# Another order of the work between two token blocks in the expert stage of a gated cross-attention and mixture-of-experts kernel

## The chip, the core and the metric

The kernel runs on one core of one Trainium2 chip. Its engines work side by side, each through its own list of instructions, and meet only at semaphores: TensorE (PE) multiplies matrices, VectorE (DVE) and GpSimd (POOL) do element-wise work, ScalarE (ACT) evaluates activation functions, SyncE (SP) issues the transfers. The metric is device time in microseconds, the median of repeated executions. A separate execution was recorded by the hardware profiler, and all rows below come from it.

## The reference, cut to what matters

A first stage (attention) makes `x` of 4096 tokens by 128. The change is in the second stage, the expert layer:

```
w = gate weights per token and expert, thresholded and normalised
h = gelu(einsum('td,edf->etf', x, W1) + b1[:, None, :])     # 8 experts, 512 hidden
eo = einsum('etf,efd->etd', h, W2) + b2[:, None, :]
out = einsum('te,etd->td', w, eo)
x = x + tanh(g_ffn[0]) * out
```

## The kernel before, in words

The expert stage goes through the tokens in NB = 8 blocks of 512. A block has CH = 32 chunks: chunk `j` is expert `e = j // 4` and quarter `f = j % 4` of its 512 hidden features. Operands are kept as a rounded part and a remainder (`_high`, `_low`), so every product takes three matmuls of 512 columns.

For each chunk there is a **first group** on PE (L1060 to L1062, three matmuls into `ps_h`, one of four buffers `j % 4`), then ACT's gelu into `h_sb` (L627, counted by `h_done`) and, for even chunks, a second gelu that writes `h_high` (L632, counted by `high_even`). DVE makes `h_high` for odd chunks by a copy (L836, `high_odd`) and `h_low` for both chunks of a pair by a subtraction (L840, `low2_done`). Then comes the **second group** on PE, `second` (L1040 to L1042), which adds the chunk's three products into `ps_y`. LAG = 4: `second(g, j - 4)` stands right behind the first group of chunk `j`. I call a first group with the second group behind it a slot.

When the four second groups of an expert are done, DVE's `combine(g, e)` (L828) adds the bias and multiplies with the token weights from `w_row`: expert 0 goes straight into `yT`, the others into `weighted`, and for these POOL adds `weighted` to `yT` (L527, counted by `added`). After the last addition of a block PE turns `yT` by four transposes (`untranspose`, L1048, into `ps_t`) and DVE's `finish` (L815) adds the residual and makes `y_out`, which SP stores.

The order on each engine is the order in which the code is written. In the kernel before, a block ends with its last four second groups back to back (chunks 28 to 31, L1067) and, on DVE, with the last two combinations (L851). The next block begins with the first groups of its chunks 0 to 3 back to back; behind the first group of chunk 2 stand the transposes of the block before, and behind DVE's pair (2, 3) stands `finish`. Blocks 0 and 1 are written out, blocks 2 to 7 are one hardware loop (`loop_b`), in which the numbers that a wait compares with are computed in registers.

The first group of chunk `j` waits for `h_done` of chunk `j - 4` from chunk 4 on. For chunks 0 to 3 the line reads

```
wait_count(pe, h_done, g * CH + (j - 3) if j >= 4 else g * CH)
```

which for chunk 0 of a block means all 32 gelus of the block before.

Of the kernel before, what the change touches and what calls it, by code (L numbers as in the profile page):

```python
# [37 lines left out]
E, FF = 8, 512  # L38
# [6 lines left out]
FC = FF // P  # L45
CH = E * FC
BT = 512
NB = TOK // BT
TPB = BT // P
LAG = 4  # L50
# [43 lines left out]
def gated_block(nc, a):  # L94
# [3 lines left out]
    with ctx:  # L98
# [3 lines left out]
        def sem(name):  # L102
            return ctx.enter_context(nc.semaphore(name))
# [168 lines left out]
        weighted_done = sem("weighted_done")  # L272
# [29 lines left out]
        def wait_count(eng, s, n):  # L302
            if not (isinstance(n, int) and n <= 0):
                eng.wait_ge(s, n)
# [20 lines left out]
        def loop_b(eng, body):  # L325

            body(0)
            body(1)
            with eng.Fori(2, NB) as g:
                body(g)  # L330
# [307 lines left out]
        def _(dve):  # L638
# [172 lines left out]
            def finish(g):  # L811

                dve.wait_ge(t_full, g + 1)
                wait_count(dve, y_stored, g * 16)
                V.tensor_tensor(y_out[:], ps_t[:, 0, :, :], x_all[:, bass.ds(g * TPB, TPB), :], ALU.add).then_inc(t_read, 1)  # L815

            def combine(g, e):

                dve.wait_ge(w2_done, g * CH + FC * (e + 1))
                dve.wait_ge(wrow_in[e % WBUF], g * (E // WBUF * 16) + 16 * (e // WBUF + 1))  # L820
                if e >= 2:
                    wait_count(dve, added, g * (E - 1) + (e - 2))
                elif e == 1:
                    wait_count(dve, added, g * (E - 1))
                else:
                    wait_count(dve, t_full, g)
                dst = yT[:] if e == 0 else weighted[:, e % 2, :]
                V.scalar_tensor_tensor(dst, ps_y[:, e % 2, :], b2_sb[:, e:e + 1], w_row[:, e % WBUF, :],  # L828
                                       ALU.add, ALU.mult).then_inc(weighted_done, 1)

            def body_b(g):
                def high(j):
                    dve.wait_ge(h_done, g * CH + (j + 1))

                    wait_count(dve, w2_done, g * CH + (j - HBUF + 1))
                    V.tensor_copy(h_high[:, j % HBUF, :], h_sb[:, j % HBUF, :]).then_inc(high_odd, 1)  # L836

                def low(j):
                    dve.wait_ge(high_odd if j % 2 else high_even, g * (CH // 2) + (j // 2 + 1))
                    V.tensor_tensor(h_low[:, j % HBUF, :], h_sb[:, j % HBUF, :], h_high[:, j % HBUF, :].bitcast(F32),  # L840
                                    ALU.subtract).then_inc(low2_done, 1)

                for j in range(0, CH, 2):
                    high(j + 1)
                    low(j)
                    low(j + 1)
                    if j == 2 and not (isinstance(g, int) and g == 0):
                        finish(g - 1)
                    if j >= FC + LAG and j % FC == 0:
                        combine(g, (j - LAG) // FC - 1)  # L850
                for e in range((CH - LAG) // FC - 1, E):  # L851
                    combine(g, e)
            loop_b(dve, body_b)
            finish(NB - 1)


        @block.tensor
        def _(pe):
# [172 lines left out]
            def second(g, j):  # L1031
                e, f = divmod(j, FC)
                if f == 0:

                    wait_count(pe, weighted_done, g * E + (e - 1) if e >= 2 else g * E)
                pe.wait_ge(high_odd if j % 2 else high_even, g * (CH // 2) + (j // 2 + 1))
                pe.wait_ge(low2_done, g * CH + (j + 1))
                dst = ps_y[:, e % 2, :]
                cols = slice(f * P, (f + 1) * P)
                mm(dst, w_high[:, E + e, cols], h_high[:, j % HBUF, :], start=(f == 0), stop=False)  # L1040
                mm(dst, w_high[:, E + e, cols], h_low[:, j % HBUF, :], start=False, stop=False)  # L1041
                mm(dst, w_low[:, E + e, cols], h_high[:, j % HBUF, :], start=False, stop=(f == FC - 1)).then_inc(w2_done, 1)  # L1042

            def untranspose(g):
                pe.wait_ge(added, (g + 1) * (E - 1))
                wait_count(pe, t_read, g)
                for t in range(TPB):
                    ins = nc.tensor.transpose(ps_t[:, 0, t, :], yT[:, t * P:(t + 1) * P], ident[:])  # L1048
                ins.then_inc(t_full, 1)

            def body_b(g):
                for j in range(CH):
                    e, f = divmod(j, FC)
                    wait_count(pe, h_done, g * CH + (j - 3) if j >= 4 else g * CH)
                    if j % 2 == 0:
                        wait_count(pe, high_even, g * (CH // 2) + (j - 4) // 2 + 1 if j >= 4 else g * (CH // 2))
                    dst = ps_h[:, j % 4, :]
                    cols = slice(f * P, (f + 1) * P)
                    xh, xl = x2_high[:, bass.ds(g * BT, BT)], x2_low[:, bass.ds(g * BT, BT)]
                    mm(dst, w_high[:, e, cols], xh, start=True, stop=False)  # L1060
                    mm(dst, w_high[:, e, cols], xl, start=False, stop=False)  # L1061
                    mm(dst, w_low[:, e, cols], xh, start=False, stop=True).then_inc(h_full, 1)  # L1062
                    if j == 2 and not (isinstance(g, int) and g == 0):
                        untranspose(g - 1)
                    if j >= LAG:
                        second(g, j - LAG)
                for j in range(CH - LAG, CH):  # L1067
                    second(g, j)
            loop_b(pe, body_b)
            untranspose(NB - 1)  # L1070


# [61 lines left out]
```

## Time and profile before

| | |
|---|---|
| median of 3 executions | 689.93 us (689.4 to 690.32) |
| the profiled execution's own time | 691.63 us |
| its span | 689.8 us |
| PE busy | 635.0 us (92%) |
| DVE busy | 534.3 us (77%) |
| ACT busy | 432.7 us (63%) |
| POOL busy | 188.1 us (27%) |
| mean granted clock of PE | 0.981 |

The first matmul of the expert stage starts at 312.22 us, the last transposes at 685.65 us, so the stage takes somewhat over half of the span. The starts of matmuls are recorded, their ends are modelled, and neighbours overlap in the record; so the time of PE is best read from the distance between starts.

### The profile page before, as it was taken

Reading aid. Unit: us, or ns where it says so; the run is one execution under the profiler, and the core shown is the slowest. Engines: PE = TensorE matmul, PEld = TensorE weight load, DVE = VectorE, ACT = ScalarE, POOL = GpSimd, SP = SyncE. Lnnn points to the kernel's source line nnn. Section 1 sums busy time; section 2 is a strip of 40 time slices with the busy share of each in tenths; the row PEclk is TensorE's granted clock in tenths of the full one; section 3 lists DMA queues with packets and bytes.
Section 4 is the critical chain, followed back from the end, with each engine's and each line's share of the span. In section 5 each row is a group of like instructions: output and inputs, shape, how many; then the busy total and the mean of one; then the engine's idle time right before and its main releaser. Section 6 shows DMA issues by size and latency. Waiting matters only on the chain.

```text
span 689.8 us, 14449 instructions
## 1 busy us (share of the span) xinstructions
PE 635.0 (92%) x3944; PEld 479.0 (69%) x3944; DVE 534.3 (77%) x1083; ACT 432.7 (63%) x764; POOL 188.1 (27%) x242
## 2 busy tenths in 40 slices
PE   2899999999999998829999999999999999999996
PEld 2566666666666666427878878878778788787784
DVE  5778888888888887544877877868868778688686
ACT  3466666666666665517757757757577677675773
POOL 6224344444433342110130220221302202212022
PEclk9999999999999999958999999999999999999999
DMA  6544344444444434102121121121111211111110
GB/s 191 135 118 121 104 115 116 113 111 117 111 110 110 110 104 104 57 0 69 46 62 48 46 62 48 46 47 61 53 54 46 61 46 46 46 61 48 58 46 15
DMA packets 48139, 52.74 MB, mean 76 GB/s; under 512 B 9329, under 2 KB 34801, under 8 KB 48113
## 3 DMA queue, kind: packets, MB, share of 16 engines
q1 hardware_dynamic: 48112, 52.42, 27.8%
q8 instruction: 13, 0.21, 0.1%
q14 instruction: 14, 0.11, 0.0%
HBM read 26.58 MB, written 2.23 MB: 42 GB/s over the span
## 4 chain that ended last, share of the span: by engine, by line
PE 79%; DVE 8%; issue 3%; POOL 3%; DMA 3%; SPq 2%; ACT 2%; DVEq 0%; POOLq 0%; ACTq 0%
PE ps_y L1040 8%; PE ps_y L1042 8%; PE ps_y L1041 8%; PE ps_h L1062 8%; PE ps_h L1060 8%; PE ps_h L1061 8%; PE scores L993 5%; PE scores L994 4%; PE scores L1001 4%; PE scores L1002 3%; POOL yT L527 3%; DVE neg_max L654 3%; PE heads L1012 3%; PE misc L881 2%; PE misc L882 2%
## 5 line engine op out<-in xcount | busy, mean ns | idle before, releaser
L627 ACT ACTIVATE h_sb<-ps_h,b_sb 128x512 f32<-128x512 f32 x256 | 175.3, 689 | 116.0 <-PE ps_h L1062 103.3
L840 DVE TENSOR_TENSOR h_low<-h_sb,h_high 128x512 fp32r<-128x512 f32 x256 | 164.4, 682 | 0.0
L527 POOL TENSOR_TENSOR yT<-yT,weighted 128x512 f32<-128x512 f32 x56 | 72.3, 1291 | 308.9 <-DVE weighted L828 308.2
L836 DVE CAST h_high<-h_sb 128x512 fp32r<-128x512 f32 x128 | 87.0, 679 | 81.4 <-ACT h_sb L627 81.3
L1040 PE MATMUL ps_y<-h_high,w_high 128*128 128x512 f32 x256 | 102.0, 399 | 4.9 <-DVE h_low L840 4.9
L1060 PE MATMUL ps_h<-x_high,w_high 128*128 (+1 forms) x256 | 101.7, 397 | 0.0
L1042 PE MATMUL ps_y<-h_high,w_low 128*128 128x512 f32 x256 | 101.4, 396 | 0.0
L1062 PE MATMUL ps_h<-x_high,w_low 128*128 (+1 forms) x256 | 101.2, 395 | 0.0
L1041 PE MATMUL ps_y<-h_low,w_high 128*128 128x512 f32 x256 | 100.7, 393 | 0.0
L1061 PE MATMUL ps_h<-x_low,w_high 128*128 (+1 forms) x256 | 100.1, 391 | 0.0
L654 DVE TENSOR_REDUCE neg_max<-scores 128x4 f32<-128x512 f32 x128 | 83.7, 685 | 14.2 <-PE scores L1002 13.1
L546 ACT ACTIVATE probs<-scores 128x512 f32<-128x512 f32 x128 | 72.9, 596 | 25.6 <-PE scores L994 23.2
L632 ACT ACTIVATE h_high<-ps_h,b_sb 128x512 fp32r<-128x512 f32 x128 | 87.5, 684 | 0.0
L560 ACT ACTIVATE part<-misc,bqk_low,low_rows_sb 128x256 fp32r<-128x256 f32 x128 | 65.5, 565 | 34.5 <-PE misc L883 34.5
L993 PE MATMUL scores<-q_masked,k_cur 128*128 128x512 f32 x128 | 60.7, 503 | 8.4 <-issue 4.7
L1001 PE MATMUL scores<-k_masked,q_stack 128*128 128x512 f32 x128 | 62.9, 521 | 3.6 <-DMA k_masked<-k_stack 3.6
L1040 PEld LDWEIGHTS ps_y<-h_high,w_high 128*128 128x128 f32 x256 | 48.0, 188 | 19.9 <-DVE h_low L840 5.7
L1061 PEld LDWEIGHTS ps_h<-x_low,w_high 128*128 128x128 f32 x256 | 48.5, 190 | 11.5
L1060 PEld LDWEIGHTS ps_h<-x_high,w_high 128*128 128x128 f32 x256 | 48.6, 190 | 11.1
L1062 PEld LDWEIGHTS ps_h<-x_high,w_low 128*128 128x128 f32 x256 | 48.3, 189 | 11.1
L1042 PEld LDWEIGHTS ps_y<-h_high,w_low 128*128 128x128 f32 x256 | 48.1, 188 | 11.0
L1041 PEld LDWEIGHTS ps_y<-h_low,w_high 128*128 128x128 f32 x256 | 48.1, 188 | 9.9
(122 smaller groups left out, 989.6 us busy)
## 6 DMA issues: line engine op xcount, KB each, us to landing
w_row<-w_scratch SPq DMA_DIRECT2D x64, 256.0 KB, 3.2
k_masked<-k_stack SPq DMA_DIRECT2D x64, 128.0 KB, 2.5
k_cur<-k_stack SPq DMA_DIRECT2D x16, 512.0 KB, 3.1
q_masked<-q_stack SPq DMA_DIRECT2D x64, 96.0 KB
w_raw<-in_w_ffn SPq DMA_DIRECT2D x16, 256.0 KB, 2.7
ctx_sb<-in_ctx SPq DMA_DIRECT2D x16, 128.0 KB, 2.1
out_y<-y_out SPq DMA_DIRECT2D x8, 256.0 KB, 3.6
probs<-in_wqk SPq DMA_DIRECT2D x2, 256.0 KB, 2.9
```

What stands on the lines that cost most here:

```text
L527: nc.gpsimd.tensor_tensor(yT[:], yT[:], weighted[:, e % 2, :], ALU.add).then_inc(added, 1)
L627: nc.scalar.activation(h_sb[:, j % HBUF, :], ps_h[:, j % 4, :], ACT.Gelu_apprx_tanh, bias=b1_sb[:, j:j + 1]).then_inc(h_done, 1)
L654: nc.vector.tensor_reduce(neg_max[:, b, ROWS * s:ROWS * s + ROWS], scores[:, 2 + s % 2, :].rearrange("p (r k) -> p r k", k=S), AX.X, ALU.m ...
L840: V.tensor_tensor(h_low[:, j % HBUF, :], h_sb[:, j % HBUF, :], h_high[:, j % HBUF, :].bitcast(F32), ALU.subtract).then_inc(low2_done, 1)
L993: mm(dst, k_cur[:, s, b * S:(b + 1) * S], q_masked[:, s, :, b * S:(b + 1) * S], start=True, stop=False)
L1001: mm(dst, q_stack[:, s, b * S:(b + 1) * S], k_masked[:, s, :, b * S:(b + 1) * S], start=True, stop=False)
L1040: mm(dst, w_high[:, E + e, cols], h_high[:, j % HBUF, :], start=(f == 0), stop=False)
L1041: mm(dst, w_high[:, E + e, cols], h_low[:, j % HBUF, :], start=False, stop=False)
L1042: mm(dst, w_low[:, E + e, cols], h_high[:, j % HBUF, :], start=False, stop=(f == FC - 1)).then_inc(w2_done, 1)
L1060: mm(dst, w_high[:, e, cols], xh, start=True, stop=False)
L1061: mm(dst, w_high[:, e, cols], xl, start=False, stop=False)
L1062: mm(dst, w_low[:, e, cols], xh, start=False, stop=True).then_inc(h_full, 1)
```

## The change

The seam between two blocks is written as every other stretch: each of the first groups of chunks 0 to 3 is followed by one of the last four second groups of the block before. The last two combinations of a block move behind DVE's pairs (0, 1) and (4, 5) of the next block, the transposes behind the second group that follows the first group of chunk 8, and `finish` behind DVE's pair (10, 11). The wait of a second group on `weighted_done` gets one formula. After the last block the rest is done outside the loop. In the changed kernel the lines below L844 lie three further down, those of the block loop on PE up to six.

```
 DVE, body_b
                     low(j + 1)
-                    if j == 2 and not (isinstance(g, int) and g == 0):
+                    later = not (isinstance(g, int) and g == 0)
+                    if j % FC == 0 and j >= FC + LAG:
+                        combine(g, (j - LAG) // FC - 1)
+                    elif j % FC == 0 and later:
+                        combine(g - 1, (j + CH - LAG) // FC - 1)
+                    if j == 2 * LAG + 2 and later:
                         finish(g - 1)
-                    if j >= FC + LAG and j % FC == 0:
-                        combine(g, (j - LAG) // FC - 1)
-                for e in range((CH - LAG) // FC - 1, E):
-                    combine(g, e)
             loop_b(dve, body_b)
+            combine(NB - 1, E - 2)
+            combine(NB - 1, E - 1)
             finish(NB - 1)
...
 PE, second
-                    wait_count(pe, weighted_done, g * E + (e - 1) if e >= 2 else g * E)
+                    wait_count(pe, weighted_done, g * E + (e - 1))
...
 PE, body_b
-                    if j == 2 and not (isinstance(g, int) and g == 0):
-                        untranspose(g - 1)
+                    later = not (isinstance(g, int) and g == 0)
                     if j >= LAG:
                         second(g, j - LAG)
-                for j in range(CH - LAG, CH):
-                    second(g, j)
+                    elif later:
+                        second(g - 1, CH + j - LAG)
+                    if j == 2 * LAG and later:
+                        untranspose(g - 1)
             loop_b(pe, body_b)
+            for j in range(CH - LAG, CH):
+                second(NB - 1, j)
             untranspose(NB - 1)
```

PE at the entry of the loop (end of block 1, begin of block 2), kernel before. `ps_y` rows are second groups, `ps_h` rows first groups; L329 and L304 are register and branch work of the sequencer.

```order
L1040 MATMUL ps_y<-h_high,w_high 128x512 [waits low2_done,high_odd]
L1041 MATMUL ps_y<-h_low,w_high 128x512
L1042 MATMUL ps_y<-h_high,w_low 128x512
L329 UNCONDITIONAL_BRANCH
L329 ISA
L304 REGISTER_ALU [waits h_done]
L1060 ISA [waits high_even]
L1060 MATMUL ps_h<-x_high,w_high 128x512
L1061 REGISTER_ALU
L1061 MATMUL ps_h<-x_low,w_high 128x512
L1062 MATMUL ps_h<-x_high,w_low 128x512
L1060 MATMUL ps_h<-x_high,w_high 128x512 [waits h_done]
```

The same place on PE in the changed kernel.

```order
L1045 MATMUL ps_y<-h_high,w_low 128x512
L329 UNCONDITIONAL_BRANCH
L329 ISA
L304 REGISTER_ALU [waits h_done]
L1063 ISA [waits high_even]
L1063 MATMUL ps_h<-x_high,w_high 128x512
L1064 REGISTER_ALU
L1064 MATMUL ps_h<-x_low,w_high 128x512
L1065 MATMUL ps_h<-x_high,w_low 128x512
L304 ISA
L1039 ISA [waits weighted_done]
L1040 ISA [waits high_even]
```

Before, the second group ahead of the branch is that of chunk 31, and a first group follows the first group. Now it is that of chunk 27, and the three sequencer instructions at the end belong to the second group of chunk 28 that comes next. The two waits ahead of the first group of chunk 0 are the same in both.

DVE from the loop's entry on, kernel before.

```order
L828 SCALAR_TENSOR_TENSOR weighted<-ps_y,b_sb,w_row 128x512 [waits added,wrow2_in,w2_done]
L828 SCALAR_TENSOR_TENSOR weighted<-ps_y,b_sb,w_row 128x512 [waits added,wrow3_in,w2_done]
L329 UNCONDITIONAL_BRANCH
L329 ISA
L304 REGISTER_ALU [waits h_done]
L836 CAST h_high<-h_sb 128x512 [waits w2_done]
L839 ISA
L840 TENSOR_TENSOR h_low<-h_sb,h_high 128x512 [waits high_even]
L840 TENSOR_TENSOR h_low<-h_sb,h_high 128x512 [waits high_odd]
```

The same place on DVE in the changed kernel.

```order
L329 UNCONDITIONAL_BRANCH
L329 ISA
L304 REGISTER_ALU [waits h_done]
L836 CAST h_high<-h_sb 128x512 [waits w2_done]
L839 ISA
L840 TENSOR_TENSOR h_low<-h_sb,h_high 128x512 [waits high_even]
L840 TENSOR_TENSOR h_low<-h_sb,h_high 128x512 [waits high_odd]
L819 ISA
L820 REGISTER_ALU [waits w2_done]
L304 ISA [waits wrow2_in]
L828 SCALAR_TENSOR_TENSOR weighted<-ps_y,b_sb,w_row 128x512 [waits added]
```

The combination of expert 6 (`wrow2_in`) has moved from ahead of the loop's begin to behind the pair (0, 1); that of expert 7 follows two pairs later.

## Rows read from the trace of the kernel before

**Rows 1.** Windows: us, busy of PE, PEld, DVE, ACT, POOL, clock, DMA.

```profile
390.00:440.00 50.00, 49.03 (x215) 39.44 (x214) 39.22 (x62) 34.06 (x54) 10.35 (x8) 1.00 0.19 53
540.00:590.00 50.00, 48.57 (x211) 38.44 (x210) 39.47 (x63) 32.20 (x50) 10.34 (x8) 1.00 0.18 52
```

**Rows 2.** Timeline of PE inside block 2: start us, duration, what.

```profile
425.17 0.39 PE L1060 MATMUL ps_h<-x_high,w_high 128*128 x1
...
447.25 0.39 PE L1060 MATMUL ps_h<-x_high,w_high 128*128 x1
```

**Rows 3.** Timeline of PE at the first seam and in the last block.

```profile
358.57 0.47 PE L1040 MATMUL ps_y<-h_high,w_high 128*128 128x512 f32 x1 [0.59 <-DVE h_low L840]
...
361.89 0.39 PE L1062 MATMUL ps_h<-x_high,w_low 128*128 128x512 f32 x1
362.55 0.66 PE L1048 MATMUL ps_t<-ident_sb,yT 128*128 128x128 f32 x4 [0.27 <-POOL yT L527]
...
681.62 0.50 PE L1040 MATMUL ps_y<-h_high,w_high 128*128 128x512 f32 x1 [0.52 <-DVE h_low L840]
```

**Rows 4.** Timeline of PE at the seam between blocks 2 and 3.

```profile
448.62 0.48 PE L1040 MATMUL ps_y<-h_high,w_high 128*128 128x512 f32 x1
448.94 0.39 PE L1041 MATMUL ps_y<-h_low,w_high 128*128 128x512 f32 x1
...
449.87 0.40 PE L1042 MATMUL ps_y<-h_high,w_low 128*128 128x512 f32 x1
450.77 0.50 PE L1040 MATMUL ps_y<-h_high,w_high 128*128 128x512 f32 x1 [0.50 <-DVE h_low L840]
451.11 0.39 PE L1041 MATMUL ps_y<-h_low,w_high 128*128 128x512 f32 x1
...
452.40 0.40 PE L1060 MATMUL ps_h<-x_high,w_high 128*128 x1
...
454.25 0.40 PE L1062 MATMUL ps_h<-x_high,w_low 128*128 x1
455.02 0.65 PE L1048 MATMUL ps_t<-ident_sb,yT 128*128 128x128 f32 x4 [0.37 <-POOL yT L527]
455.43 0.48 PE L1060 MATMUL ps_h<-x_high,w_high 128*128 x1
455.75 0.40 PE L1061 MATMUL ps_h<-x_low,w_high 128*128 x1
```

**Rows 5.** Timeline of POOL at the seams.

```profile
359.77 2.73 POOL L527 TENSOR_TENSOR yT<-yT,weighted 128x512 f32<-128x512 f32 x2 [2.23 <-DVE weighted L828]
...
448.55 1.28 POOL L527 TENSOR_TENSOR yT<-yT,weighted 128x512 f32<-128x512 f32 x1 [4.23 <-DVE weighted L828]
...
453.60 1.29 POOL L527 TENSOR_TENSOR yT<-yT,weighted 128x512 f32<-128x512 f32 x1 [0.16 <-DVE weighted L828]
```

**Rows 6.** Timeline of ACT, the gelu of chunk 31 of block 2.

```profile
448.14 0.69 ACT L627 ACTIVATE h_sb<-ps_h,b_sb 128x512 f32<-128x512 f32 x1
```

**Rows 7.** Timeline of PE's weight loads, end of block 2.

```profile
448.61 0.19 PEld L1040 LDWEIGHTS ps_y<-h_high,w_high 128*128 128x128 f32 x1 [0.25 <-issue]
```

**Rows 8.** Timeline of DVE around the same seam.

```profile
447.65 0.74 DVE L828 SCALAR_TENSOR_TENSOR weighted<-ps_y,b_sb,w_row 128x512 f32<-128x512 f32 x1
448.86 1.26 DVE L836 CAST h_high<-h_sb 128x512 fp32r<-128x512 f32 x1 [0.47 <-ACT h_sb L627]
...
458.85 0.68 DVE L815 TENSOR_TENSOR y_out<-ps_t,x_all 128x512 f32<-128x512 f32 x1
459.45 0.41 DVE L836 CAST h_high<-h_sb 128x512 fp32r<-128x512 f32 x1
...
467.51 0.43 DVE L836 CAST h_high<-h_sb 128x512 fp32r<-128x512 f32 x1 [0.47 <-ACT h_sb L627]
```

**Rows 9.** DMA queues: whole execution, then 470 to 689 us: packets, MB, share.

```profile
q8 instruction: 13, 0.21, 0.1%
...
q1 hardware_dynamic: 7957, 10.64, 16.0%
```

## The prediction

> **What bounds the kernel now.** I read the windows first [rows 1]. Inside the expert stage PE is busy 49.03 of 50 us at clock 1.00, DVE 39.22, ACT 34.06, POOL 10.35. The reader sees that PE is the engine to count, and that DVE has a fifth of its time free (10.78 of 50 us).
>
> Then the timeline of PE. From the first group of chunk 15 of block 2 to that of chunk 31 lie 16 slots, 96 matmuls, in 447.25 - 425.17 = 22.08 us [rows 2]: 0.230 us per matmul, 1.38 us per slot, with no gap. No instruction order makes this shorter. A block of 192 matmuls is 44.16 us. From the second group of chunk 30 in block 0 to the same one in block 7 lie seven blocks, 681.62 - 358.57 = 323.05 us [rows 3], 46.15 us per block. So 1.99 us per block lie at the seam, and there are seven seams.
>
> The seam between blocks 2 and 3 shows of what they are made, as starts minus the 0.23 us that is normal [rows 4]: the second group of chunk 28 (448.62 to 448.94) 0.09; the wait of chunk 30 for its `h_low` (449.87 to 450.77) 0.67, and its restart (to 451.11) 0.11; the wait of the transposes for POOL's last addition (454.25 to 455.02) 0.54; the transposes themselves (455.02 to 455.43) 0.41; the restart behind them 0.09. That is 1.91. From 451.11 to 452.40 five matmuls take 1.29 instead of 1.15: 0.14 more, around the first jump back of the loop. At the first seam the transposes wait 0.66 - 0.23 = 0.43 [rows 3].
>
> Why these waits: four second groups back to back last 2.8 us, and chunk 31's gelu, copy and subtractions don't come that fast; and the transposes come 2.8 us behind the last second group, while a combination and additions of 1.29 us [rows 5] lie between.
>
> **What the change removes.** Both waits and the late chunk 28. Of the 1.99 us per block the transposes and the restart behind them stay (0.50), which leaves 1.49; I leave 0.05 for pitches that only look removable, and take 1.44 us x 7 = 10.1 us. No matmul, gelu, addition or transfer is added or taken away.
>
> **What it adds, slot by slot.** (a) The first group of chunk 0 waits for all gelus of the block before, also chunk 31's. So far four second groups lay between; now only that of chunk 27. In the seam read above chunk 31's gelu ends at 448.14 + 0.69 = 448.83 [rows 6]. The first matmul of the new block would start at 448.63, where the second group of chunk 28 starts now. How late is a late start? That second group's weight load came at 448.61 [rows 7], 0.02 us ahead of the matmul's normal start instead of 0.23, and it cost 0.09; so the loss is the load's start, less the matmul's normal start, plus 0.11. Chunk 30 agrees: 450.77 - 450.10 + 0.11 = 0.78, measured 0.67 + 0.11. What remains is the time from the gelu's end to the load. POOL's addition that ends at 359.77 + 2.73 = 362.50 released PE at 362.55 where waits compare with constants [rows 3, 5]: 0.05. In the loop the one that ends at 454.89 released it at 455.02 [rows 4, 5]: 0.13, with one register instruction that waits. Chunk 0 has two of these in a row, so my estimate is 0.05 + 2 x 0.08 = 0.21. Loss at a loop seam: 448.83 + 0.21 - 448.63 + 0.11 = 0.52; at the first seam, with constants, 0.36. Sum: 6 x 0.52 + 0.36 = 3.5 us. Bounds: below, 0.2 per seam (only the gelu's lateness, nothing for the release), 1.4; above, 1.0 per seam, if the sequencer, which has nothing queued ahead after a wait, costs as much again, 7.0. I take 3.5, since each part of it has a row.
>
> (b) Behind this stall the sequencer has three register instructions ahead of the second group of chunk 28 and one or two per group for the next three. They are hidden when it runs ahead of PE; freshly stalled it may not. Estimate 0.05 x 6 = 0.3, bounds 0 and 6 x 0.14 = 0.8, by the five slow matmuls behind 451.11 [rows 4].
>
> (c) The transposes now stand at the end of slot 8, after `combine` of expert 7 at the usual place, behind pair (4, 5). The steady pattern tells the time of POOL's addition: the combination of expert 5 starts at 447.65 [rows 8], in slot 31, and its addition runs 448.55 to 449.83 [rows 5], so it ends 1.20 us into the next slot. The last addition then ends 1.20 us into slot 8, the transposes' weight load would go at 1.15 and is released at 1.25, still ahead of the matmul's own 1.38. By the rule in (a) that costs nothing; I take 0.03 x 7 = 0.2. Bounds 0 and 0.1 per seam. This is a near miss: 0.2 us more anywhere on DVE or POOL would show here.
>
> (d) DVE. Behind a combination POOL's addition runs, and the next copy takes 1.26 instead of 0.43 us [rows 8]. Two such pairs, 2 x 0.83 us per seam, move to where DVE has work. The same pattern runs in every other four chunks of the block, at full pace of PE, with 0.47 us idle ahead of the copy [rows 8]; so it costs 0. `finish` (0.60 us from start to start, 458.85 to 459.45 [rows 8]) stands where no addition runs: `combine` of expert 0 writes `yT` itself, and the copy behind it takes 0.43 [rows 8]. The 0.83 saved there holds it. Cost 0; if that cover were gone, DVE would be 0.6 late, and a second group waits only for `h_low` of four chunks before.
>
> (e) The wait on `weighted_done`: the second group of expert 0 no longer asks for expert 7's combination, and that of expert 1 (slot 8) does; the combination ends in slot 7, as in every steady expert. On SP the store waits for `finish`, 8 chunks later; behind it is only the load of expert 5's `w_row`, which waits for a later combination anyway. After the last block everything is as before, apart from the loop's exit, which now lies between the second groups of chunks 27 and 28: bounds 0 and 0.14, taken 0.
>
> **Sum**: -10.1 + 3.5 + 0.3 + 0.2 = -6.1 us. The profiled span goes from 689.8 to 683.7, its own time from 691.63 to 685.5. That execution lies 1.70 above the median of the runs, and a difference carries over: 689.93 - 6.1 = 683.8 us.
>
> **A rule weighed against the trace.** A copy that meets an addition takes 1.26 us and ends shortly after it, 450.12 against 449.83 [rows 5, 8]; the subtractions behind it are not lengthened. The Trainium skill, page "SBUF — State Buffer", section "SBUF: two separate sides", says that VectorE's two-port operations and GpSimd share a port pair under an exclusive lock, and that whoever comes second is blocked entirely. The trace agrees for the copies. By that rule each seam gains two collisions where there were none, which is case 5 below.
>
> **The rivals.** *The stall is cheaper (case 2).* The release to a waiting sequencer takes no longer than 0.05 and the restart is part of it: 0.2 per seam, 1.4 us in all, with (b) and (c) at nothing: 689.93 - 8.7 = 681.2. For it speaks that the load can be queued while the branch runs; against it the 0.13 of the register case.
>
> *The loop's turn comes out into the open (case 3).* Jump, register setup and waits stood under four second groups and a wait of 0.67; now they stand between two groups that PE wants back to back. If they cost 1.0 per seam, 7 x 1.0 + 0.5 = 7.5, and 10.1 - 7.5 = 2.6: 687.3. For it: 0.14 was lost at the one jump that can be seen. Against it: the later ones lose nothing before the transposes, and from 470 to 689 us there is no instruction fetch in the queues (only the data queue is listed, while the whole execution has 13 packets on the queue q8) [rows 9]. The Trainium skill, page "Runtime: NRT & Kernel Launch", section "Instruction fetch mechanics", says that a taken branch outside the fetched pages stalls for a fetch; with four jumps back in that stretch and no fetch, the trace does not bear this out for this loop.
>
> *Nothing changes (case 4).* The stall is as long as what was removed: 10.1 / 7 = 1.44 per seam. It needs a release of 1.1 us from the gelu's end; no row shows one above 0.13. 689.9.
>
> *Slower (case 5).* DVE becomes the bound through the collisions: 14 copies, each 0.83 longer, on the path. 14 x 0.83 = 11.6, less 6.1, is 5.5 more: 695.4. It decides once DVE's free time in four chunks is used up, 0.216 x 5.52 = 1.2 us by the windows [rows 1]. For it: the near miss in (c). Against it: the steady chunks already hold one collision in every four at PE's pace.
>
> **How the numbers follow.** The forecast (gain of 4.4 to 7.6 us, so 682.3 to 685.5) 0.62; case 2 0.14; case 3 0.15; case 4 0.05; case 5 0.04. About 0.2% (1.4 us) is what can be told from no change. Faster: the first three, 0.91 less a little of case 3, 0.90; same 0.05; slower 0.05. The range leaves out the ends of cases 2 and 3 and the last two: 681.5 to 686.8.
>
> **What would show it right or wrong.** In the changed profile: blocks 45.3 us apart instead of 46.15; the idle time of the second group on `h_low` gone except in the first and last block; a new idle time ahead of the first group of chunk 0, put down to ACT's gelu, about 0.3 us in the record and 0.5 from start to start; transposes with next to no wait, 0.41 long; `finish` without lateness for the next copy; DVE's waits for `h_sb` no longer than in steady chunks. The prediction is wrong if the wait at chunk 0 is above 1 us, if PE waits for `h_low` or `weighted_done` in slots 0 to 12, or if the pitch of 1.38 us changes elsewhere.

## The result, and the profile after

| | before | after |
|---|---|---|
| median | 689.93 us (689.4 to 690.32) | 685.74 us (683.78 to 686.28) |
| profiled span | 689.8 us | 682.0 us |
| start of the expert stage's first matmul | 312.22 us | 309.48 us |
| from there to the last transpose | 373.8 us | 368.7 us |

Both medians are of five executions. The ratio is 0.9936, 95% interval 0.992 to 0.9952: 4.4 us faster, between 3.3 and 5.5 (the two medians themselves lie 4.2 us apart). The two profiled executions differ by more (7.8 us), because the attention stage, which nothing touched, took 2.7 us less in the second; over all traces of this study the expert stage begins anywhere from 309.5 to 313.2 us. I therefore compare the expert stage by itself: 5.1 us shorter.

The clock is not the difference. The expert stage begins at a granted clock of 0.50 (1.2 GHz). In the stretch ahead of it at the same clock PE was busy 5.4 of 16.6 us before and 4.0 of 14.4 us after. The clock is 1.00 (2.4 GHz) from 316.1 us on before and from 312.1 us on after, up to the end of the stage. From the first group of chunk 0 to that of chunk 12 in block 0 lie 16.61 us before and 16.67 us after.

The windows of the changed kernel (columns as in [rows 1]):

```profile
390.00:440.00 50.00, 49.73 (x217) 40.05 (x217) 41.31 (x63) 34.35 (x54) 10.28 (x8) 1.00 0.16 50
540.00:590.00 50.00, 49.73 (x217) 40.00 (x216) 41.58 (x64) 34.83 (x54) 10.32 (x8) 1.00 0.16 52
```

PE is busy 0.7 to 1.2 us more of each 50, DVE 2.1. What PE waited for in the kernel before and in the changed one (engine, tile and line, releaser: us in total, times, longest):

```profile
PE ps_t L1048 <- POOL yT L527: 5.1, 8, 2.4
PE ps_y L1040 <- DVE h_low L840: 4.9, 9, 0.7
```

```profile
PE ps_t L1051 <- POOL yT L527: 2.3, 1, 2.3
PE ps_h L1063 <- ACT h_sb L627: 1.6, 6, 0.3
PE ps_y L1043 <- DVE h_low L840: 1.5, 2, 0.8
```

Both old waits are gone from the seven seams (what is left lies in the first and last block), and the forecast new one stands there, six times (at the first seam it is too short for this list). The seam ahead of block 3, which answers to [rows 4], and the first seam, which answers to [rows 3]; PE's timeline after:

```profile
353.65 0.39 PE L1045 MATMUL ps_y<-h_high,w_low 128*128 128x512 f32 x1
354.12 0.50 PE L1063 MATMUL ps_h<-x_high,w_high 128*128 128x512 f32 x1
354.46 0.40 PE L1064 MATMUL ps_h<-x_low,w_high 128*128 128x512 f32 x1
...
444.19 0.39 PE L1045 MATMUL ps_y<-h_high,w_low 128*128 128x512 f32 x1
444.85 0.49 PE L1063 MATMUL ps_h<-x_high,w_high 128*128 x1 [0.27 <-ACT h_sb L627]
445.18 0.40 PE L1064 MATMUL ps_h<-x_low,w_high 128*128 x1
...
457.21 0.39 PE L1045 MATMUL ps_y<-h_high,w_low 128*128 128x512 f32 x1
457.46 0.66 PE L1051 MATMUL ps_t<-ident_sb,yT 128*128 128x128 f32 x4
457.87 0.48 PE L1063 MATMUL ps_h<-x_high,w_high 128*128 x1
458.19 0.40 PE L1064 MATMUL ps_h<-x_low,w_high 128*128 x1
```

In the loop the stall at chunk 0 is (0.66 - 0.23) + (0.33 - 0.23) = 0.53 us, at the first seam 0.24 + 0.11 = 0.35. The transposes start 0.02 us late (0.25 from 457.21 to 457.46). ACT's gelu of chunk 31, which answers to [rows 6], and PE's weight load behind it, one fence each:

```profile
443.92 0.69 ACT L627 ACTIVATE h_sb<-ps_h,b_sb 128x512 f32<-128x512 f32 x1
```

```profile
444.84 0.19 PEld L1063 LDWEIGHTS ps_h<-x_high,w_high 128*128 128x128 f32 x1 [0.70 <-issue]
```

From the gelu's end, 444.61, to the load, 444.84, are 0.23 us.

### The profile page after: what moved, and what is told of

Same layout as the page of the kernel before. It is cut to its first block, busy times and chain, and to the rows that moved or that the text cites. A ratio compares the mean times of both kernels' runs of the same rounds, so it can differ in the third digit from the quotient of the medians.

```text
span 682.0 us, 14455 instructions
## 1 busy us (share of the span) xinstructions
PE 635.3 (93%) x3944; PEld 480.7 (70%) x3944; DVE 546.0 (80%) x1083; ACT 434.5 (64%) x764; POOL 188.1 (28%) x242
## 4 chain that ended last, share of the span: by engine, by line
PE 84%; DVE 7%; issue 2%; ACT 2%; DMA 2%; SPq 1%; POOL 0%; DVEq 0%; POOLq 0%; ACTq 0%
PE ps_h L1063 9%; PE ps_h L1065 8%; PE ps_y L1043 8%; PE ps_h L1064 8%; PE ps_y L1044 8%; PE ps_y L1045 8%; PE scores L996 5%; PE scores L997 4%; PE scores L1004 4%; PE scores L1005 3%; DVE neg_max L654 3%; PE heads L1015 3%; PE misc L884 2%; PE misc L886 2%; PE misc L885 2%
## 5 line engine op out<-in xcount | busy, mean ns | idle before, releaser
L836 DVE CAST h_high<-h_sb 128x512 fp32r<-128x512 f32 x128 | 98.7, 771 | 68.5 <-ACT h_sb L627 68.5
L1063 PE MATMUL ps_h<-x_high,w_high 128*128 (+1 forms) x256 | 103.1, 403 | 1.9 <-ACT h_sb L627 1.6
L1064 PE MATMUL ps_h<-x_low,w_high 128*128 (+1 forms) x256 | 100.2, 391 | 0.0
L1063 PEld LDWEIGHTS ps_h<-x_high,w_high 128*128 128x128 f32 x256 | 48.5, 189 | 16.6 <-issue 4.8
L1065 PEld LDWEIGHTS ps_h<-x_high,w_low 128*128 128x128 f32 x256 | 48.3, 189 | 11.4
L1064 PEld LDWEIGHTS ps_h<-x_low,w_high 128*128 128x128 f32 x256 | 48.5, 189 | 10.9
```

## The experiments

Medians differ from session to session by some tenths, so each ratio is against runs of the kernel before on the same chip. "Stage" runs from the first matmul of the expert stage to the last transpose in the profiled execution.

| run | median, us | ratio to before (95%) | stage, us |
|---|---|---|---|
| changed kernel again | 684.71 | 0.992 (0.990 to 0.994) | 368.4 |
| changed, exact waits | 681.46 | 0.9865 (0.984 to 0.9889) | 364.4 |
| changed, exact waits, again | 681.38 | 0.9864 (0.9838 to 0.989) | 364.9 |
| before, only the turn moved | 691.75 | 1.0023 (1.0009 to 1.0038) | 375.2 |
| the same, one gelu short | 688.65 | 0.9978 (0.9959 to 0.9998) | 372.7 |
| changed, turn in slot 7 | 696.11 | 1.0078 (1.0053 to 1.0103) | 377.3 |
| changed, small additions | 682.09 | 0.9894 (0.9866 to 0.9922) | 365.6 |
| before, exact waits | 690.21 | 1.0006 (0.9988 to 1.0024) | 374.1 |
| exact waits, no transposes | 677.23 | 0.9822 (0.9773 to 0.9871) | 359.9 |

**Exact waits.**

```
-                    wait_count(pe, h_done, g * CH + (j - 3) if j >= 4 else g * CH)
+                    wait_count(pe, h_done, g * CH + (j - 3))
                     if j % 2 == 0:
-                        wait_count(pe, high_even, g * (CH // 2) + (j - 4) // 2 + 1 if j >= 4 else g * (CH // 2))
+                        wait_count(pe, high_even, g * (CH // 2) + (j - 4) // 2 + 1)
```

> The changed kernel, but the first group of chunks 0 to 3 waits for the gelus of chunk j-4 alone, as every other chunk does, and not for all of the block before. Theory (the slot account: each seam costs the stall at chunk 0 plus the transposes, and nothing else): the stall of 0.53 us at six seams and 0.35 at the first goes, blocks come 44.9 us apart instead of 45.43, the time falls by 3.5 us against the changed kernel, to about 682.2. Rival A (the wait only covers another one, DVE's combination or h_low of chunk 28 to 31 being late too): PE then waits at the second groups of slots 0 to 3 and gains less than 1 us. Rival B (DVE is the real bound through the copies that meet POOL's additions): no gain, and DVE's waits for gelus vanish. The pitch inside a slot is open: it was 1.380 us in seven of eight blocks of the kernel before and 1.387 in all blocks of the changed one, in the two traces I have; if the stall at chunk 0 sets it, it returns to 1.380 and another 1.4 us are gained.

Measured: 681.46 us, 3.3 below the changed kernel of the same session and 8.7 below the kernel before. The seam ahead of block 4, PE:

```profile
490.50 0.40 PE L1045 MATMUL ps_y<-h_high,w_low 128*128 128x512 f32 x1
490.74 0.39 PE L1063 MATMUL ps_h<-x_high,w_high 128*128 x1
490.97 0.39 PE L1064 MATMUL ps_h<-x_low,w_high 128*128 x1
```

No gap is left (0.24 and 0.23 us). The stage is 4.3 us shorter than in the first trace of the changed kernel; 3.5 was the stall, and most of the rest is a shorter pitch of the slots in five of the eight blocks (see the two pitches below). Nothing stood behind this wait, and rivals A and B are out. The same edit in the old order:

> The kernel before with the exact waits of the first groups of chunks 0 to 3 (as in the run with the changed kernel, where they gave 0.53 us per seam). Theory (in the old order four second groups lie between chunk 31's gelu and the new block, so the loose wait had long been met): no change, 690.1 within 0.6. Rival (the sequencer's wait on registers at the loop's begin costs by itself, however early the count is reached): some tenths of a us per seam faster, 688 to 689.5.

Measured: no change (690.21 against 690.3), and PE's waits are as they were:

```profile
PE ps_t L1048 <- POOL yT L527: 5.1, 8, 2.4
PE ps_y L1040 <- DVE h_low L840: 4.8, 9, 0.6
```

So the loose wait costs nothing where four second groups cover it. It was the interleaving that laid it open.

**Only the turn moved** (on the kernel before).

```
+                    if j >= LAG:
+                        second(g, j - LAG)
-                    if j == 2 and not (isinstance(g, int) and g == 0):
+                    if j == 2 * LAG and not (isinstance(g, int) and g == 0):
                         untranspose(g - 1)
-                    if j >= LAG:
-                        second(g, j - LAG)
...
-                    if j == 2 and not (isinstance(g, int) and g == 0):
-                        finish(g - 1)
...
+                    if j == 2 * LAG + 2 and not (isinstance(g, int) and g == 0):
+                        finish(g - 1)
```

> The kernel before, with only the transposes (behind the second group in the slot of chunk 8) and the residual (behind DVE's pair 10, 11) moved; the last four second groups and the last two combinations stay at the block's end. Theory (slot account): PE's wait for POOL's last addition goes, 0.43 to 0.61 us per seam, on average 0.55, in all 3.8 us; the wait for h_low of chunk 30 and its restart (0.78) and the late chunk 28 (0.09) stay. Blocks 45.6 us apart, time 689.9 - 3.8 = 686.1. Rival (the two waits are one: the second swallows the lateness of the first, so that taking one away lets something else wait): less than 1 us. If moving the turn alone brings what the whole change brought (4.2 us), the interleaving brought nothing.

Measured: 691.75 us, 1.6 slower than before. The expectation failed. The wait for POOL did go. The timelines of PE, ACT and DVE, a fence each, at the seam ahead of block 3:

```profile
453.64 0.39 PE L1060 MATMUL ps_h<-x_high,w_high 128*128 x1
...
456.87 0.39 PE L1062 MATMUL ps_h<-x_high,w_low 128*128 x1
457.76 0.47 PE L1040 MATMUL ps_y<-h_high,w_high 128*128 128x512 f32 x1 [0.51 <-ACT h_high L632]
```

```profile
454.62 0.69 ACT L627 ACTIVATE h_sb<-ps_h,b_sb 128x512 f32<-128x512 f32 x1 [4.41 <-PE ps_h L1062]
455.21 0.68 ACT L632 ACTIVATE h_high<-ps_h,b_sb 128x512 fp32r<-128x512 f32 x1
455.78 1.27 ACT L627 ACTIVATE h_sb<-ps_h,b_sb 128x512 f32<-128x512 f32 x2
```

```profile
456.58 0.43 DVE L836 CAST h_high<-h_sb 128x512 fp32r<-128x512 f32 x1 [1.90 <-ACT h_sb L627]
456.93 1.28 DVE L840 TENSOR_TENSOR h_low<-h_sb,h_high 128x512 fp32r<-128x512 f32 x2
```

From the first group of chunk 0 (453.64) to its second group (457.76) are 4.12 us: gelu, second gelu, gelu of chunk 1, copy, subtraction, in this order. Five first groups last only 3.45. In the kernel before, waiting and transposes stretched this distance, from 452.40 [rows 4] to

```profile
456.91 0.40 PE L1040 MATMUL ps_y<-h_high,w_high 128*128 128x512 f32 x1
```

which is 4.51, and the chain fitted in. Wait and transposes together were hiding another wait, of 0.66 us from start to start, which is more than the wait for POOL (0.54). By the starts this makes a seam of the loop about 0.1 us longer, 0.6 to 0.8 us in all. The stage grew by 1.3 us (373.82 to 375.16); the rest is a longer pitch of the slots (see below), which held in five blocks here and in one before. So the traces show that the edit gains nothing; how much of the 1.6 us is its doing they leave open. To test the chain, the second gelu of chunk 0 was cut short (64 of 512 columns, blocks 1 to 7; the rest is left out):

```
+                        n = 64 if j == 0 and not (isinstance(g, int) and g == 0) else BT
-                        nc.scalar.activation(h_high[:, j % HBUF, :], ps_h[:, j % 4, :], ACT.Gelu_apprx_tanh,
+                        nc.scalar.activation(h_high[:, j % HBUF, 0:n], ps_h[:, j % 4, 0:n], ACT.Gelu_apprx_tanh,
```

> The run with only the turn moved, in which PE waited 0.66 us at the second group of chunk 0 (put down to ACT's second gelu), with that second gelu of chunk 0 cut from 512 to 64 columns in blocks 1 to 7 (the other columns keep old values). Theory (after five first groups back to back PE waits for the chain gelu, second gelu, gelu of chunk 1, copy, subtraction; the wait for POOL had covered it): the chain is 0.4 to 0.5 us shorter, the wait falls to about 0.2, and the time by 2.8 to 3.5 us against the turn alone, to 688.3 to 689. Rival (the wait there is the combination's or the loop's): no change against the turn alone, 691.7.

Measured: 688.65 us, 3.1 less (the stage is 2.5 us shorter). From start to start the wait is 0.32 us, half of what it was; ACT and PE at the same place (lines one further down):

```profile
452.16 0.30 ACT L633 ACTIVATE h_high<-ps_h,b_sb 128x64 fp32r<-128x64 f32 x1
```

```profile
453.79 0.39 PE L1063 MATMUL ps_h<-x_high,w_low 128*128 x1
454.34 0.47 PE L1041 MATMUL ps_y<-h_high,w_high 128*128 128x512 f32 x1 [0.16 <-ACT h_high L633]
```

**Turn in slot 7** (on the changed kernel: `if j == 2 * LAG - 1 and later: untranspose(g - 1)`).

> The changed kernel with the transposes one slot earlier, behind the second group in the slot of chunk 7. Theory (the last addition ends 1.20 us into slot 8, and the transposes in the changed kernel come just behind that): PE now stands at the beginning of slot 8 and waits about 1.20 + 0.13 us for POOL, 1.2 to 1.3 us per seam, 8.4 to 9.1 us in all: 694.1 to 694.8. Rival (the additions are done much earlier and the place in slot 8 has slack to spare): no change, 685.7.

Measured: 696.11 us, 11.4 above the changed kernel of the same session and more than expected, though the stage grew by 8.6 to 8.9 us, as forecast. What the rest of the median is, no trace shows. PE's timeline in block 3:

```profile
460.27 0.39 PE L1045 MATMUL ps_y<-h_high,w_low 128*128 128x512 f32 x1
461.88 0.66 PE L1051 MATMUL ps_t<-ident_sb,yT 128*128 128x128 f32 x4 [1.22 <-POOL yT L527]
```

The wait is 1.61 - 0.23 = 1.38 us. POOL's last addition there:

```profile
460.57 1.26 POOL L527 TENSOR_TENSOR yT<-yT,weighted 128x512 f32<-128x512 f32 x1 [4.26 <-DVE weighted L828]
```

It ends at 461.83, and the transposes' weight load starts at 461.88. The last addition does end just ahead of the place that the change chose; one slot earlier would have cost more than the whole change gives.

**Small additions** (on the changed kernel; 8 of 512 columns, the rest of the sum is left out).

```
-                    nc.gpsimd.tensor_tensor(yT[:], yT[:], weighted[:, e % 2, :], ALU.add)
+                    nc.gpsimd.tensor_tensor(yT[:, 0:8], yT[:, 0:8], weighted[:, e % 2, 0:8], ALU.add)
```

> The changed kernel with each of POOL's additions to yT cut from 512 to 8 columns (the rest of the sum over experts is left out); all waits and orders stay. The copies on DVE then meet next to no addition. Theory (the 14 additional meetings of copies with additions lie in DVE's free time, as the prediction said): all copies take 0.43 us, DVE's busy time falls by about 7 x 8 x 0.8 = 45 us, the seams keep their stall of 0.53 us and their transposes, and only the very end gains, where two additions of 1.29 us stand between the last combination and the last transposes: 2.3 us less than the changed kernel, 682.4 to 683.4. Rival (the port: what the collisions cost DVE reaches PE in part): blocks come less than 45.3 us apart and the time is below 681.5.

Measured: 682.09 us. Groups of the copies (count, busy us, mean ns, idle before) in the changed kernel, then here:

```profile
L836 DVE CAST h_high<-h_sb 128x512 fp32r<-128x512 f32 x128 | 98.7, 771 | 68.5 <-ACT h_sb L627 68.5
```

```profile
L836 DVE CAST h_high<-h_sb 128x512 fp32r<-128x512 f32 x128 | 54.7, 428 | 110.5 <-ACT h_sb L627 110.5
```

All that the copies save, 44 us, turns into idle time of DVE (42 us more). Blocks are 45.17 or 45.37 us apart, against 45.25 or 45.44 in the changed kernel's second trace. The difference of 0.08 is not the copies' but the transposes', which here start without lateness:

```profile
457.46 0.39 PE L1045 MATMUL ps_y<-h_high,w_low 128*128 128x512 f32 x1
457.69 0.60 PE L1051 MATMUL ps_t<-ident_sb,yT 128*128 128x128 f32 x4
458.05 0.48 PE L1063 MATMUL ps_h<-x_high,w_high 128*128 x1
```

(0.59 us from 457.46 to 458.05, where the changed kernel has 0.66.) The time is 0.3 us below what was expected; the longer pitch (next) held in four blocks only.

**The changed kernel again, and two pitches.**

> The changed kernel again, to see what repeats. Theory: 685.7 within 0.5 us, seams with the same stalls of 0.53 us, blocks 45.43 us apart and the slower pitch of 1.387 us per slot in all blocks (if the order fixes it). Rival: the pitch inside a slot changes from execution to execution, and with it the time by about 1.5 us. A third: the attention stage differs from execution to execution by 1 to 3 us (the expert stage began at 312.2 us in the one trace and at 309.5 us in the other), which would be the scatter of the runs.

Measured: 684.71 us, 1.0 below the first median and so outside the 0.5 that was expected, with the same seams. What changed was the pitch. In the first trace of the changed kernel, first groups of chunks 15 and 31 of block 2, to be held against [rows 2]:

```profile
420.85 0.40 PE L1063 MATMUL ps_h<-x_high,w_high 128*128 x1
...
443.03 0.40 PE L1063 MATMUL ps_h<-x_high,w_high 128*128 x1
```

22.18 us instead of 22.08. Averaged over chunks 12 to 30 a slot takes either 1.3800 or 1.3867 us, nothing between, and keeps it until the block ends or turns. The longer pitch held in 1 of 8 blocks before, in 3 of 8 in the second trace of the old order (the one with exact waits), in 8 of 8 in the first trace of the changed kernel, in 6 of the second. The next run asks what sets it (the exact-wait kernel without `untranspose` at chunk 8; the outputs of blocks 0 to 6 are left out; DVE's `finish` reads `x_all` in place of `ps_t` there, and its waits on the transposes become waits on the additions):

```
-                    if j == 2 * LAG and later:
-                        untranspose(g - 1)
```

> The kernel with exact waits, without the transposes of blocks 0 to 6 (only the last block is turned, and the output of the others is left out; DVE and SP do the same amount of work). PE then has nothing at a seam. Theory (slot account): the 0.53 us per seam of transposes and restart go, 3.7 us in all, 677.8. What is open is the pitch of a slot, which was 1.380 in some blocks and 1.387 us in others of nearly every trace, and changed only between two blocks. Theory R (it is set anew whenever PE restarts, after a stall or after the transposes): without any restart all eight blocks show one pitch, and it is the one that the stage's head sets. Theory L (the loop's turn or another engine changes it): the pitch still changes from block to block.

Measured: 677.23 us (four executions, 675.95 to 682.11), 4.2 below the exact waits, and 1.3800 in all eight blocks. The first groups of chunk 0 of blocks 3 and 4 lie exactly 192 x 0.230 us apart (their first matmul is L1064 here):

```profile
444.52 0.39 PE L1064 MATMUL ps_h<-x_high,w_high 128*128 x1
...
488.68 0.39 PE L1064 MATMUL ps_h<-x_high,w_high 128*128 x1
```

This fits theory R, that the pitch is drawn anew when PE restarts or changes to the transposes; one trace without restarts is not a proof. The exact-wait kernel again:

> The kernel with exact waits again, for the version that beats both. Theory: 681.5 within 0.7 us, faster than the kernel before by 8 to 9 us, no idle time of PE at any seam. If the order of the instructions fixed the pitch, it would be 1.387 in blocks 0 to 2 and 1.380 in blocks 3 to 7 as in the first trace; I expect another pattern.

Measured: 681.38 us, and another pattern of pitches (the longer one in blocks 0 to 2 and 4 to 7, where the first trace had it in 0 to 2). So the order doesn't fix it. The three traces with the new order and exact waits show more: the pitch went unchanged through every jump back of the loop, and where it changed (once in the first trace, twice in the one just measured, never in the one without transposes) it did so right behind the transposes. That speaks against the loop's turn, for theory R. What draws the one or the other value stays open.

## Why the prediction was right

The direction, the mechanism and the full range (681.5 to 686.8) held; the point, 683.8 us, was 1.9 us too low, and the forecast gain of 6.1 us lies outside the measured interval of 3.3 to 5.5. The median of 685.74 also lies 0.2 us above the narrower range of the forecast case, between it and case 3; that the case was the forecast one and not case 3 is told by the trace alone. And one sign of being wrong that the prediction names came true: the pitch changed elsewhere. Step by step:

- *Bound.* PE, at 0.230 us per matmul: right, down to the block without a turn at 44.16 us.
- *Removed, 1.44 us per seam.* Right in its sum. But I took the parts as independent, and they aren't. The wait for POOL (0.54) is worth nothing alone, because behind it the chain of chunk 0 is late by 0.66. The interleaving removes the second one too: it puts second groups between the first groups, so that from the first group of chunk 0 to its second group lie four slots and a first group, 6.2 us, for a chain of 4.1.
- *(a) Stall at chunk 0*, 0.52 and 0.36: measured 0.53 and 0.35; release 0.21, measured 0.23 at all six loop seams. The exact waits bought it back, 3.3 us by the medians.
- *(b) Sequencer behind the stall*, 0.3 in all: nothing of it in the trace. Slot 1 of each block has the steady pitch.
- *(c) Transposes*, 0.03 per seam on top of the 0.50 counted as staying: measured 0.02 + 0.41 + 0.09 = 0.52 in the loop, and 0.45 at the first two seams, so nothing in sum. The near miss was real: transposes that wait for nothing cost 0.44 per seam (small additions), so the lateness costs 0.08 in the loop, but 0.06 of it was already in the 0.50. The last addition ends 1.36 us into slot 8 instead of 1.20 (456.12 + 1.29 = 457.41; the slot begins at 456.05).
- *(d) DVE*, 0: right. DVE's busy time grew by 546.0 - 534.3 = 11.7 us, which is the forecast 14 x 0.83, and none of it reached PE. Case 5 is refuted, case 4 too.
- *Case 3* (the loop's turn exposed) would have shown as a longer stall in the loop than (a). There is none.

The term that is missing is the pitch. I took "no gap" for "fixed". Against the trace of before, seven more blocks of 31 or 32 slots ran 0.0067 us longer, about 1.5 us. With what was measured in place of (b) and (c), the stage should have shrunk by 10.1 - 3.5 = 6.6 us, and with the pitch by 5.1; measured 5.1. That it was seven blocks is in part chance: the pitch differs between executions of one kernel, and two traces of each order (1 and 3 blocks, 8 and 6) don't tell whether the new order makes the longer one more frequent. The medians say 4.2 and 5.4 us in two sessions, with scatter from the attention stage on top.

## What to carry to other kernels

A wait that is met early costs nothing and so is easily left looser than its buffer needs. When work is moved closer, go through every count that the moved instructions wait for: here the one loose count took back 3.3 us, two fifths of what the new order could give.

The length of a stall on the bounding engine is no price tag. Before counting one as a gain, follow the next instructions with that stall gone and ask whose data is then late; moving the transposes alone gained nothing (the median rose by 1.6 us), and together with the interleaving it gained 4 to 5.

## What the runs showed of the hardware

- TensorE ran the same stream of matmuls at granted clock 1.00 with either 1.3800 or 1.3867 us per six, constant between one wait or group of transposes and the next, different from block to block and from execution to execution; in three traces without a stall at the seams it changed only right behind transposes; in the one of them without transposes between blocks it stayed at 1.3800.
- A matmul whose weight load is released late costs 0.1 us beyond the wait; the rule of the prediction (load's start, less the matmul's normal start, plus 0.11) gives 444.84 - 444.42 + 0.11 = 0.53 for the new stall, as measured. For transposes it gives too much: 457.46 - 457.44 + 0.11 = 0.13, measured 0.08.
- What a release of PE costs depends on what the wait stands on, and not on the count being computed. At chunk 0 in the loop two waiting register instructions stand ahead of the weight load, which started 0.23 us after the end of the gelu; at the first seam, with constants, it was 0.05. One such instruction stood ahead of the transposes in the kernel before: 0.13 from the end of the addition. In the changed kernel and in the run with the turn in slot 7 none stands there in the loop, though the count comes from a register: 0.05 (461.83 to 461.88).
